# Adjacency layer with residual and layer norm: the bias enters through the self half's cross product, taken by VectorE

## Chip, cores and metric

The kernel runs on one core of a Trainium2 chip. The metric is the device time of one execution in microseconds (us); less is better. A core has TensorE (PE: matmuls, with the weight loads listed apart as PEld), VectorE (DVE), ScalarE (ACT), GpSimd (POOL), SyncE (SP, which only issues DMAs here) and 16 DMA engines.

## What is computed

The reference, cut to what matters (x is 8 x 2048 x 512, adj is 2048 x 2048 of 0 and 1, W is 512 x 1024, all results fp32):

```python
Wi, Wj = (W[:, :Din], W[:, Din:])
mi = jnp.einsum('bkd,od->bko', x, Wi)
mj = jnp.einsum('bkd,od->bko', x, Wj)
deg = a.sum(axis=1)                      # a = adj as float
out = deg[None, :, None] * (mi + b) + jnp.einsum('ij,bjo->bio', a, mj)
return _layernorm(x + out, axis=-1)
```

So there are two projections of x, the neighbour half (mj, h = 0 in the kernel) and the self half (mi, h = 1). The bias b is added to mi before it is multiplied by the degrees.

## The kernel before

The 8 batches of 2048 rows are 128 tiles of 128 rows, 16 to a batch. Each batch has two stages.

**Projection.** TensorE runs its matmuls on numbers of reduced precision, so each operand is cut in a top part and a rest, and three products are made. For tile n and half h, `project(n, s, h, first)` makes 4 matmuls into `cross_ps[h]` (from `x_df` and `W_df`) and then 8 into `main_ps[h]`. The result is main * (1 + 1/S) - cross. There is one PSUM bank for each of `main_ps[0]`, `main_ps[1]`, `cross_ps[0]`, `cross_ps[1]`. ScalarE copies the cross product out (`take_cross(n, 0)`, `take_cross(n, 1)`, into `cross[0]`, `cross[1]`), and VectorE combines (`combine_mj`, `combine_mi`). The neighbour half stays on the chip in `mj_hi` (made by ScalarE) and `mj_lo` (made by GpSimd). The self half goes through one SBUF tile `mi`, which SyncE stores to DRAM (`store_mi`, to `mi_dram`); the next write of `mi` waits until that store has landed (`mi_stored`). VectorE also splits x two tiles ahead (`split_x(n + 2)`: `x_top`, `x_raw`), ScalarE makes `x_hi` and `x_lo` of it (`parts`), and GpSimd `x_df` (`difference`).

**Aggregation.** For each of 16 output tiles TensorE makes 32 matmuls of a widened adjacency tile (`adjT`, by ScalarE's `widen`) with `mj_hi` and `mj_lo` into one of two banks `agg_ps`. SyncE loads `mi` and x back (`mi_in`, `r`), GpSimd adds the bias (`add_bias`), VectorE forms deg * mi + x (`residual`), adds the aggregate and normalises (`normalise`).

**Batch 0** has more to do. The weights come in eight chunks, which VectorE and ScalarE split (`split_w`, `copy_w_hi`), and tiles 0 and 1 (`NATIVE = 2`) are projected "natively" from the unsplit fp32 data, since they can start early. Their self halves are copied out of PSUM by `native_mi(0)` and `native_mi(1)`, on ScalarE, tile 0 from `main_ps[1]` and tile 1 from `cross_ps[1]`. The first split tile is tile 2. Its self-half cross product writes `cross_ps[1]` again, so TensorE waits there for `mi_ready` to reach 2, which is for both native copies (here `h` is 1):

```python
if first:
    pe.wait_ge(mj_ready if h == 0 else mi_ready, NATIVE)
```

Batch 0 also takes in the adjacency matrix, 64 chunks of 128x512 integers in four buffers `adj_in`. Of each chunk ScalarE makes an int8 copy (`cast_chunk`) and VectorE a running sum of degrees (`count_chunk`, `deg_part`); 28 chunks go in the projection stage, two for each tile from tile 2 on, and 36 in the aggregation stage.

Every engine runs its own instruction stream in the written order, and semaphores tie the streams together. SyncE's stream around the two native tiles is: for n in 0, 1: wait for the native matmuls, `load_chunk(2 + n)`, `store_mi(n)`.

Of the kernel before, what the change touches and what calls it, by code (L numbers as in the profile page):

```python
# [5 lines left out]
def bass_adj_resnorm(nc, x, xt, adjt, wt, b, out):  # L6
# [6 lines left out]
    ALU = mybir.AluOpType  # L13
# [5 lines left out]
    P = 128  # L19
# [4 lines left out]
    GT = 4  # L24
# [15 lines left out]
    with ctx:  # L40
# [65 lines left out]
        x_parts_ready = sem("x_parts_ready")  # L106
        x_df_ready = sem("x_df_ready")
        cross_done = sem("cross_done")
        cross_ready = sem("cross_ready")
        main_done = sem("main_done")  # L110
        mj_ready = sem("mj_ready")
        mj_hi_ready = sem("mj_hi_ready")
# [9 lines left out]
        deg_ready = sem("deg_ready")  # L122
        adjT_ready = sem("adjT_ready")
        zeroed = sem("zeroed")
        mib_ready = sem("mib_ready")
        res_ready = sem("res_ready")
        agg_done = sem("agg_done")
        sum_ready = sem("sum_ready")
# [42 lines left out]
        def _(sp):  # L171
# [13 lines left out]
            sp.dma_start(x_first[1], xt[1]).then_inc(x_first_loaded[1], 16)  # L185
            for c in range(DK):
                sp.dma_start(w_stage[c][:, :], wt[c]).then_inc(w_loaded[c], 16)
            for s in range(2):
                sp.dma_start(x_raw[s][:, :], xt[NATIVE + s]).then_inc(x_loaded[s], 16)
            sp.dma_start(bias[:, :], b.partition_broadcast(P)).then_inc(b_loaded, 16)  # L190
            for c in range(2):
                load_chunk(c)
            for n in range(NATIVE):
# [80 lines left out]
        @block.gpsimd  # L274
        def _(pool):
            pool.memset(warm[:, :], 0.0).then_inc(zeroed, 1)
            pool.memset(ones[:, :].bitcast(fp32), 1.0).then_inc(zeroed, 1)

            def difference(n, s):
                pool.wait_ge(x_parts_ready, 2 * (n - NATIVE) + 2)  # L280
                pool.tensor_tensor(x_df[s][:, :], x_top[:, :], x_lo[s][:, :].bitcast(fp32),  # L281
                                   ALU.subtract).then_inc(x_df_ready, 1)

            def rest_of_mj(n, t):
                pool.wait_ge(mj_hi_ready, n + 1)
                pool.tensor_tensor(mj_lo[:, bass.ds(t, 1), :].rearrange("p t d -> p (t d)"), mj[:, :],  # L286
                                   mj_hi[:, bass.ds(t, 1), :].rearrange("p t d -> p (t d)").bitcast(fp32),
                                   ALU.subtract).then_inc(mj_lo_ready, 1)

            def add_bias(m, u, turn):  # L290
                pool.wait_ge(mi_loaded[u % 2], turn)
                pool.tensor_tensor(mi_in[u % 2][:, :], mi_in[u % 2][:, :], bias[:, :], ALU.add).then_inc(mib_ready, 1)  # L292

            difference(NATIVE, 0)

            def batch(bt):
                zero = known(bt) and bt == 0
                final = known(bt) and bt == NB - 1

                def proj(g):  # L300
                    for u in range(GT):
                        if zero and GT * g + u < NATIVE:
                            continue
                        n = NT * bt + GT * g + u
                        if not (final and known(g) and g == NG - 1 and u == GT - 1):
                            difference(n + 1, (u + 1) % 2)
                        rest_of_mj(n, GT * g + u)

                over_groups(pool, zero, final, proj)
                if zero:  # L310
                    pool.wait_ge(b_loaded, 16)
                with pool.Fori(0, NP) as k:
                    for u in range(2):
                        add_bias(NT * bt + 2 * k + u, u, 16 * (NP * bt + k + 1))

            over_batches(pool, batch)

        @block.tensor
        def _(pe):
# [12 lines left out]
            def project(n, s, h, first):  # L332
                half = 1 - h
                if first:
                    pe.wait_ge(w_ready, (h + 1) * DK)
                if h == 0:
                    pe.wait_ge(x_df_ready, n - NATIVE + 1)
                if first:
                    pe.wait_ge(mj_ready if h == 0 else mi_ready, NATIVE)
                else:  # L340
                    pe.wait_ge(cross_ready, 2 * (n - NATIVE) - 1 + h)
                for k in range(DK):
                    last = nc.tensor.matmul(cross_ps[h][:, :], x_df[s][:, k * P:(k + 1) * P],  # L343
                                            W_df[:, half * DK + k, :], start=(k == 0), stop=(k == DK - 1))
                last.then_inc(cross_done, 1)
                if first:
                    pe.wait_ge(w_hi_ready, (h + 1) * DK)
                    pe.wait_ge(w_lo_ready, (h + 1) * DK)
                pe.wait_ge(mj_ready if h == 0 else mi_ready, n)
                for k in range(DK):  # L350
                    nc.tensor.matmul(main_ps[h][:, :], x_hi[s][:, k * P:(k + 1) * P],  # L351
                                     W_hi[:, half * DK + k, :], start=(k == 0), stop=False)
                    last = nc.tensor.matmul(main_ps[h][:, :], x_lo[s][:, k * P:(k + 1) * P],  # L353
                                            W_lo[:, half * DK + k, :], start=False, stop=(k == DK - 1))
                last.then_inc(main_done, 1)
# [66 lines left out]
        def _(act):  # L422
# [6 lines left out]
                nc.scalar.activation(mj_hi[:, n, :], (main_ps if n == 0 else cross_ps)[0][:, :],  # L429
                                     ACT.Copy).then_inc(mj_hi_ready, 1)  # L430

            def native_mi(n):
                act.wait_ge(main_done, NATIVE + n + 1)
                if n:
                    act.wait_ge(mi_stored, 16 * n)
                nc.scalar.activation(mi[:, :], (main_ps if n == 0 else cross_ps)[1][:, :],
                                     ACT.Copy).then_inc(mi_ready, 1)

            def parts(n, s):
                act.wait_ge(x_top_ready, n - NATIVE + 1)  # L440
                if not (known(n) and n < NATIVE + 2):
# [6 lines left out]
                act.wait_ge(x_parts_ready, 2 * (n - NATIVE) - 2)  # L448
                act.dma_start(x_raw[s][:, :], xt[n]).then_inc(x_loaded[s], 16)

            def take_cross(n, h):
                act.wait_ge(cross_done, 2 * (n - NATIVE) + 1 + h)
                act.wait_ge(mj_ready if h == 0 else mi_ready, n)
                nc.scalar.activation(cross[h][:, :], cross_ps[h][:, :], ACT.Copy).then_inc(cross_ready, 1)  # L454

            def top_of_mj(n, t):
                act.wait_ge(mj_ready, n + 1)
# [23 lines left out]
            native_mj_hi(1)  # L481
            parts(NATIVE, 0)
            load_x(NATIVE + 2, 0)
            native_mi(0)
            for order in range(1, DK):
                copy_w_hi(order, DK + order)
            native_mi(1)

            def batch(bt):
                zero = known(bt) and bt == 0  # L490
# [2 lines left out]
                def proj(g):  # L493
                    last_group = known(g) and g == NG - 1
                    for u in range(GT):
                        t = GT * g + u
                        n = NT * bt + t
                        if zero and t < NATIVE:
                            continue
                        if not (final and last_group and u == GT - 1) and (zero or not (known(g) and t == 0)):  # L500
                            parts(n + 1, (u + 1) % 2)
                        take_cross(n, 0)
                        if not (final and last_group and u >= GT - 3):
                            load_x(n + 3, (u + 1) % 2)
                        if zero:
                            for c in proj_chunks(t)[:-1]:
                                cast_chunk(c)
                        take_cross(n, 1)
                        top_of_mj(n, t)
                        if zero:  # L510
                            cast_chunk(proj_chunks(t)[-1])
                        if last_group and u in (0, 2):
                            widen(u // 2, u // 2, NT if zero else None)
# [37 lines left out]
        def _(dve):  # L551
# [29 lines left out]

            def combine_mj(n):
                dve.wait_ge(main_done, 2 * n + 1)
                dve.wait_ge(cross_ready, 2 * (n - NATIVE) + 1)
                if not (known(n) and n == NATIVE):
                    dve.wait_ge(mj_lo_ready, n - NATIVE)
                nc.vector.scalar_tensor_tensor(mj[:, :], main_ps[0][:, :], 1.0 + 1.0 / S, cross[0][:, :],  # L587
                                               ALU.mult, ALU.subtract).then_inc(mj_ready, 1)

            def combine_mi(n):  # L590
                dve.wait_ge(main_done, 2 * n + 2)
                dve.wait_ge(cross_ready, 2 * (n - NATIVE) + 2)
                dve.wait_ge(mi_stored, 16 * n)
                nc.vector.scalar_tensor_tensor(mi[:, :], main_ps[1][:, :], 1.0 + 1.0 / S, cross[1][:, :],  # L594
                                               ALU.mult, ALU.subtract).then_inc(mi_ready, 1)
# [18 lines left out]
                                      deg_ps[:, 0:2 * TPB].rearrange("p (t c) -> p t c", c=2)[:, :, 0]  # L614
                                      ).then_inc(deg_ready, 1)

            def residual(m, i, u, turn):
                dve.wait_ge(mib_ready, m + 1)
                dve.wait_ge(r_loaded[u], turn)
                if known(m) and m < NT:  # L620
                    dve.wait_ge(deg_ready, m // TPB + 1)
# [34 lines left out]
            split_x(NATIVE, 0, 16)  # L656
            for order in range(1, DK):
                split_w(order, DK + order)
            split_x(NATIVE + 1, 1, 16)

            def batch(bt):
                zero = known(bt) and bt == 0
# [2 lines left out]
                def proj(g):  # L665
                    for u in range(GT):
# [7 lines left out]
                        if zero:  # L674
                            for c in proj_chunks(t)[:-1]:
                                count_chunk(c)
                        combine_mi(n)
                        if zero:
                            count_chunk(proj_chunks(t)[-1])
# [2 lines left out]

                over_groups(dve, zero, final, proj)
                base = NT * bt
                residual(base, 0, 0, 16 * (NG * bt + 1))

                def agg(g):
                    for u in range(GT):
# [10 lines left out]
                                take_degrees(3)  # L699
                        ending = known(g) and g == NG - 1 and u == GT - 1  # L700
                        if not ending:
                            residual(m + 1, i + 1, (u + 1) % GT, 16 * (NG * bt + g + 1 + (u + 1) // GT))
                        normalise(m, u, u % 2, final and ending)

                if zero:
# [39 lines left out]
```

## Time and profile before

| | before |
|---|---|
| time, median of 3 runs | 1643.62 us (1643.59 to 1643.74) |
| the profiled execution's own time | 1643.72 us |
| its span in the profile | 1641.9 us |
| TensorE busy | 1634.2 us, 7196 matmuls |
| VectorE busy | 844.8 us, 1879 instructions |
| ScalarE busy | 661.7 us, 964 instructions |
| GpSimd busy | 498.4 us, 386 instructions |
| DMA | 187.27 MB, mean 114 GB/s |

The span runs from the first to the last instruction of the profiled execution; the 1.8 us between it and that execution's time lie around the instructions. Busy time counts instructions that do work, not waits. A matmul of 512 columns shows as 389 ns, but the next one starts 0.23 us later, since they are pipelined. Batch 0's projection ends at about 97 us of the span and its aggregation at about 214 us; each later batch takes 87 us of projection and 116 us of aggregation.

### The profile page before, as it was taken

To read this page: it belongs to the slowest core of one execution; us is meant where nothing else is said; L and a number is where in the kernel's file an instruction comes from. 1 tells how busy PE (TensorE), PEld (TensorE's weight loads), DVE (VectorE), ACT (ScalarE), POOL (GpSimd) and SP (SyncE) were. 2 spreads that over 40 slices of the span, in tenths; PEclk is the share of its full clock that TensorE was granted. 3 is DMA by queue.
4 is the path that set the end of the run, shared out by engine and by line. 5 is a ranking of instruction groups with operands and counts; after the bars stand their busy time and mean duration, and the time that the engine had idled before them with its cause. 6 is when DMAs were issued, how large, how long until landed. Compare 5 with 4: busy or idle time off the path is not lost.

```text
span 1641.9 us, 24654 instructions
## 1 busy us (share of the span) xinstructions
PE 1634.2 (100%) x7196; PEld 1346.8 (82%) x7196; DVE 844.8 (51%) x1879; ACT 661.7 (40%) x964; POOL 498.4 (30%) x386
## 2 busy tenths in 40 slices
PE   9999999999999999999999999999999999999998
PEld 6888888888888888888888888888888888888886
DVE  8787644554444544444544544444544454544544
ACT  5765445332453324532245332452325522255221
POOL 3532134311343114431144211442114421144210
PEclk9999999999999999999999999999999999999999
DMA  6676422332234323243223332233323333233332
GB/s 205 193 226 223 141 84 94 131 108 96 83 102 133 100 93 96 89 134 109 84 95 101 123 115 83 95 114 117 102 83 102 124 106 106 74 101 115 96 115 70
DMA packets 102843, 187.27 MB, mean 114 GB/s; under 512 B 11424, under 2 KB 11680, under 8 KB 102816
## 3 DMA queue, kind: packets, MB, share of 16 engines
q1 hardware_dynamic: 84672, 154.05, 29.1%
q10 hardware_dynamic: 18144, 32.91, 6.3%
q8 instruction: 11, 0.18, 0.0%
q14 instruction: 16, 0.13, 0.0%
HBM read 119.80 MB, written 67.11 MB: 114 GB/s over the span
## 4 chain that ended last, share of the span: by engine, by line
PE 98%; DVE 1%; DMA 0%; issue 0%; POOL 0%; ACT 0%; DVEq 0%
PE agg_ps L375 57%; PE cross_ps L343 14%; PE main_ps L351 14%; PE main_ps L353 14%; DVE W_lo L558 0%; DVE W_df L561 0%; DMA mi_in<-in_wt 0%; DVE adjT L555 0%; DVE x_raw L579 0%; DVE mj_lo L568 0%; PE deg_ps L360 0%; POOL x_df L281 0%; DVE x_top L576 0%; DVE stats L630 0%; DVE r L628 0%
## 5 line engine op out<-in xcount | busy, mean ns | idle before, releaser
L375 PE MATMUL agg_ps<-mj_hi,adjT 128*128 128x512 f32 x2048 | 797.0, 389 | 0.0
L375 PE MATMUL agg_ps<-mj_lo,adjT 128*128 128x512 f32 x2048 | 796.7, 389 | 0.0
L470 ACT ACTIVATE adjT<-adjT 128x2048 fp32r (+1 forms) x128 | 245.4, 1917 | 562.8 <-PE agg_ps L375 562.8
L375 PEld LDWEIGHTS agg_ps<-mj_hi,adjT 128*128 128x128 f32 x2048 | 384.5, 188 | 79.9
L375 PEld LDWEIGHTS agg_ps<-mj_lo,adjT 128*128 128x128 f32 x2048 | 384.3, 188 | 79.7
L351 PE MATMUL main_ps<-W_hi,x_hi 128*128 128x512 f32 x1008 | 392.3, 389 | 0.0
L353 PE MATMUL main_ps<-W_lo,x_lo 128*128 128x512 f32 x1008 | 392.1, 389 | 0.0
L292 POOL TENSOR_TENSOR mi_in<-mi_in,bias 128x512 f32<-128x512 f32 x128 | 166.9, 1307 | 649.9 <-DMA mi_in<-mi_dram 649.9
L628 DVE TENSOR_TENSOR r<-agg_ps,r 128x512 f32<-128x512 f32 x128 | 88.6, 692 | 355.0 <-PE agg_ps L375 354.9
L343 PE MATMUL cross_ps<-W_df,x_df 128*128 128x512 f32 x1008 | 270.2, 390 | 0.6 <-DVE W_df L561 0.5
L286 POOL TENSOR_TENSOR mj_lo<-mj,mj_hi 128x512 f32 (+1 forms) x126 | 166.7, 1323 | 323.4 <-ACT mj_hi L458 323.4
L454 ACT ACTIVATE cross<-cross_ps 128x512 f32<-128x512 f32 x252 | 148.6, 590 | 215.0 <-PE cross_ps L343 213.5
L343 PEld LDWEIGHTS cross_ps<-W_df,x_df 128*128 128x128 f32 x1008 | 189.0, 188 | 40.9 <-DVE W_df L561 0.9
L351 PEld LDWEIGHTS main_ps<-W_hi,x_hi 128*128 128x128 f32 x1008 | 189.3, 188 | 39.8 <-DVE mi L594 0.3
L353 PEld LDWEIGHTS main_ps<-W_lo,x_lo 128*128 128x128 f32 x1008 | 189.1, 188 | 39.2
L281 POOL TENSOR_TENSOR x_df<-x_top,x_lo 128x512 fp32r<-128x512 f32 x126 | 164.9, 1309 | 150.1 <-ACT x_lo L445 149.8
L587 DVE SCALAR_TENSOR_TENSOR mj<-main_ps,cross 128x512 f32<-128x512 f32 x126 | 87.1, 691 | 224.0 <-PE main_ps L353 218.8
L594 DVE SCALAR_TENSOR_TENSOR mi<-main_ps,cross 128x512 f32<-128x512 f32 x126 | 87.0, 691 | 107.6 <-PE main_ps L353 105.7
L622 DVE SCALAR_TENSOR_TENSOR r<-mi_in,deg,r 128x512 f32<-128x512 f32 x128 | 101.4, 796 | 13.1 <-POOL mi_in L292 9.2
L443 ACT ACTIVATE x_hi<-x_top 128x512 fp32r<-128x512 f32 x126 | 79.6, 632 | 63.3 <-PE main_ps L353 61.3
L630 DVE BATCH_NORM_STATS2 stats<-r 128x6 f32<-128x512 f32 x128 | 89.0, 695 | 11.7
L579 DVE TENSOR_TENSOR x_raw<-x_raw,x_top 128x512 f32<-128x512 f32 x126 | 87.3, 693 | 4.3
(59 smaller groups left out, 592.1 us busy)
## 6 DMA issues: line engine op xcount, KB each, us to landing
mi_dram<-mi SPq DMA_DIRECT2D x128, 256.0 KB, 2.1
mi_in<-mi_dram SPq DMA_DIRECT2D x128, 256.0 KB, 2.7
r<-in_x SPq DMA_DIRECT2D x128, 256.0 KB, 2.6
out<-r SPq DMA_DIRECT2D x127, 256.0 KB, 2.1
x_raw<-in_xt ACTq DMA_DIRECT2D x124, 256.0 KB, 2.7
adj_in<-in_adjt SPq DMA_DIRECT2D x64, 256.0 KB, 3.9
r<-in_wt SPq DMA_DIRECT2D x4, 256.0 KB, 5.2
adj_in<-in_xt SPq DMA_DIRECT2D x2, 256.0 KB, 4.0
```

The source lines that it names most:

```text
L281: pool.tensor_tensor(x_df[s][:, :], x_top[:, :], x_lo[s][:, :].bitcast(fp32), ALU.subtract).then_inc(x_df_ready, 1)
L286: pool.tensor_tensor(mj_lo[:, bass.ds(t, 1), :].rearrange("p t d -> p (t d)"), mj[:, :], mj_hi[:, bass.ds(t, 1), :].rearrange("p t d -> p ...
L292: pool.tensor_tensor(mi_in[u % 2][:, :], mi_in[u % 2][:, :], bias[:, :], ALU.add).then_inc(mib_ready, 1)
L343: last = nc.tensor.matmul(cross_ps[h][:, :], x_df[s][:, k * P:(k + 1) * P], W_df[:, half * DK + k, :], start=(k == 0), stop=(k == DK - 1))
L351: nc.tensor.matmul(main_ps[h][:, :], x_hi[s][:, k * P:(k + 1) * P], W_hi[:, half * DK + k, :], start=(k == 0), stop=False)
L353: last = nc.tensor.matmul(main_ps[h][:, :], x_lo[s][:, k * P:(k + 1) * P], W_lo[:, half * DK + k, :], start=False, stop=(k == DK - 1))
L375: last = nc.tensor.matmul(agg_ps[s][:, :], adjT[s][:, j, :], part[:, j, :], start=(j == 0 and part is mj_hi), stop=(j == NT - 1 and part i ...
L454: nc.scalar.activation(cross[h][:, :], cross_ps[h][:, :], ACT.Copy).then_inc(cross_ready, 1)
L470: nc.scalar.activation(adjT[s][:, :, :], adjT8[:, :, bass.ds(i * P, P)], ACT.Copy).then_inc(adjT_ready, 1)
L622: nc.vector.scalar_tensor_tensor(r[u][:, :], mi_in[u % 2][:, :], deg[:, bass.ds(i, 1)], r[u][:, :], ALU.mult, ALU.add).then_inc(res_ready, 1)
L628: nc.vector.tensor_tensor(r[u][:, :], agg_ps[s][:, :], r[u][:, :], ALU.add).then_inc(sum_ready, 1)
L630: nc.vector.bn_stats(stats[:, :], r[u][:, :]).then_inc(ln_step, 1)
```

## The change

The bias no longer is added by GpSimd when `mi` has come back from DRAM. For the split tiles VectorE, and not ScalarE, takes the self half's cross product out of PSUM, and subtracts the bias as it does so; since the result is main minus cross, the stored `mi` then holds the bias. For the two native tiles VectorE, and not ScalarE, copies `mi` out of PSUM and adds the bias. GpSimd's loop of 128 adds and its semaphore `mib_ready` are gone, and `residual` waits for the load of `mi_in` itself. The semaphore `cross_ready` becomes one for each half. The load of the bias is issued two DMAs earlier. No matmul is added, removed or moved.

```diff
@@ SyncE, start
             for c in range(DK):
                 sp.dma_start(w_stage[c][:, :], wt[c]).then_inc(w_loaded[c], 16)
+            sp.dma_start(bias[:, :], b.partition_broadcast(P)).then_inc(b_loaded, 16)
             for s in range(2):
                 sp.dma_start(x_raw[s][:, :], xt[NATIVE + s]).then_inc(x_loaded[s], 16)
-            sp.dma_start(bias[:, :], b.partition_broadcast(P)).then_inc(b_loaded, 16)
@@ GpSimd
-            def add_bias(m, u, turn):
-                pool.wait_ge(mi_loaded[u % 2], turn)
-                pool.tensor_tensor(mi_in[u % 2][:, :], mi_in[u % 2][:, :], bias[:, :], ALU.add).then_inc(mib_ready, 1)
...
-                if zero:
-                    pool.wait_ge(b_loaded, 16)
-                with pool.Fori(0, NP) as k:
-                    for u in range(2):
-                        add_bias(NT * bt + 2 * k + u, u, 16 * (NP * bt + k + 1))
@@ TensorE, project
                 else:
-                    pe.wait_ge(cross_ready, 2 * (n - NATIVE) - 1 + h)
+                    pe.wait_ge(cross_ready[h], n - NATIVE)
@@ ScalarE
-            def native_mi(n):
-                act.wait_ge(main_done, NATIVE + n + 1)
-                if n:
-                    act.wait_ge(mi_stored, 16 * n)
-                nc.scalar.activation(mi[:, :], (main_ps if n == 0 else cross_ps)[1][:, :],
-                                     ACT.Copy).then_inc(mi_ready, 1)
...
-                        take_cross(n, 0)
+                        take_cross(n)
...
-                        take_cross(n, 1)
                         top_of_mj(n, t)
@@ VectorE
+            def native_mi(n):
+                if n == 0:
+                    dve.wait_ge(b_loaded, 16)
+                else:
+                    dve.wait_ge(mi_stored, 16 * n)
+                dve.wait_ge(main_done, NATIVE + n + 1)
+                nc.vector.tensor_tensor(mi[:, :], (main_ps if n == 0 else cross_ps)[1][:, :], bias[:, :],
+                                        ALU.add).then_inc(mi_ready, 1)
+
+            def take_cross_less_bias(n):
+                dve.wait_ge(cross_done, 2 * (n - NATIVE) + 2)
+                dve.wait_ge(mi_ready, n)
+                nc.vector.tensor_tensor(cross[1][:, :], cross_ps[1][:, :], bias[:, :],
+                                        ALU.subtract).then_inc(cross_ready[1], 1)
...
-            def residual(m, i, u, turn):
-                dve.wait_ge(mib_ready, m + 1)
+            def residual(m, i, u, turn, mi_turn):
+                dve.wait_ge(mi_loaded[u % 2], mi_turn)
...
             for order in range(1, DK):
                 split_w(order, DK + order)
+            native_mi(0)
             split_x(NATIVE + 1, 1, 16)
+            native_mi(1)
...
                         if zero:
                             for c in proj_chunks(t)[:-1]:
                                 count_chunk(c)
+                        take_cross_less_bias(n)
                         combine_mi(n)
```

What stands where, as the two built programs have it. The first place is VectorE's stream at the start, from the split of the last weight chunk to the first `mj`. "L555" is a line of the kernel that the row belongs to, `adjT` in the top parts of the weights is their scratch space, and `mi<-main_ps` and `mi<-cross_ps` are the native copies. Before:

```order
L555 TENSOR_SCALAR adjT<-r 128x2x256 [waits w_loaded3]
L558 TENSOR_TENSOR W_lo<-r,adjT 128x512 [waits w_top_ready]
L561 SCALAR_TENSOR_TENSOR W_df<-adjT,W_lo 128x512 [waits w_lo_ready]
L576 TENSOR_SCALAR x_top<-x_raw 128x512 [waits x_df_ready,x_parts_ready,x_loaded1]
L579 TENSOR_TENSOR x_raw<-x_raw,x_top 128x512 [waits x_top_ready]
L587 SCALAR_TENSOR_TENSOR mj<-main_ps,cross 128x512 [waits cross_ready,main_done]
```

And of the changed kernel (its line numbers are its own):

```order
L535 TENSOR_SCALAR adjT<-r 128x2x256 [waits w_loaded3]
L538 TENSOR_TENSOR W_lo<-r,adjT 128x512 [waits w_top_ready]
L541 SCALAR_TENSOR_TENSOR W_df<-adjT,W_lo 128x512 [waits w_lo_ready]
L576 TENSOR_TENSOR mi<-main_ps,bias 128x512 [waits main_done,b_loaded]
L556 TENSOR_SCALAR x_top<-x_raw 128x512 [waits x_df_ready,x_parts_ready,x_loaded1]
L559 TENSOR_TENSOR x_raw<-x_raw,x_top 128x512 [waits x_top_ready]
L576 TENSOR_TENSOR mi<-cross_ps,bias 128x512 [waits main_done,mi_stored]
L567 SCALAR_TENSOR_TENSOR mj<-main_ps,cross 128x512 [waits cross_ready0,main_done]
```

The two native copies now stand on VectorE behind all eight weight chunks, one before and one behind the split of tile 3's x, and the second waits for the store of the first.

The second place is VectorE's stream over one tile of batch 0 (tile 3). Before:

```order
L587 SCALAR_TENSOR_TENSOR mj<-main_ps,cross 128x512 [waits mj_lo_ready,cross_ready,main_done]
L576 TENSOR_SCALAR x_top<-x_raw 128x512 [waits x_df_ready,x_parts_ready,x_loaded1]
L579 TENSOR_TENSOR x_raw<-x_raw,x_top 128x512 [waits x_top_ready]
L608 TENSOR_TENSOR deg_part<-deg_part,adj_in 128x512 [waits deg_part_ready,adj_loaded2]
L594 SCALAR_TENSOR_TENSOR mi<-main_ps,cross 128x512 [waits mi_stored,cross_ready,main_done]
L608 TENSOR_TENSOR deg_part<-deg_part,adj_in 128x512 [waits deg_part_ready,adj_loaded3]
```

And of the changed kernel:

```order
L567 SCALAR_TENSOR_TENSOR mj<-main_ps,cross 128x512 [waits mj_lo_ready,cross_ready0,main_done]
L556 TENSOR_SCALAR x_top<-x_raw 128x512 [waits x_df_ready,x_parts_ready,x_loaded1]
L559 TENSOR_TENSOR x_raw<-x_raw,x_top 128x512 [waits x_top_ready]
L603 TENSOR_TENSOR deg_part<-deg_part,adj_in 128x512 [waits deg_part_ready,adj_loaded2]
L582 TENSOR_TENSOR cross<-cross_ps,bias 128x512 [waits mi_ready,cross_done]
L589 SCALAR_TENSOR_TENSOR mi<-main_ps,cross 128x512 [waits mi_stored,cross_ready1,main_done]
L603 TENSOR_TENSOR deg_part<-deg_part,adj_in 128x512 [waits deg_part_ready,adj_loaded3]
```

One instruction is added, between the two degree counts. Later batches have the same stream without the counts.

## Rows read from the trace of the kernel before

**Rows 1.** The page: busy us (share of the span) and instructions of each engine

```profile
PE 1634.2 (100%) x7196; PEld 1346.8 (82%) x7196; DVE 844.8 (51%) x1879; ACT 661.7 (40%) x964; POOL 498.4 (30%) x386
```

**Rows 2.** Waits of the weight loads: us in total, times, longest

```profile
PEld cross_ps L343 <- DVE W_df L561: 0.9, 1, 0.9
PEld cross_ps L343 <- POOL x_df L281: 0.5, 1, 0.5
...
PEld main_ps L351 <- DVE mi L594: 0.3, 1, 0.3
```

**Rows 3.** Timeline of the start: start us, us, engine, line, what

```profile
20.91 0.58 ACT L436 ACTIVATE mi<-cross_ps 128x512 f32<-128x512 f32 x1
20.97 0.39 PE L353 MATMUL main_ps<-W_lo,x_lo 128*128 128x512 f32 x1
21.09 0.69 DVE L561 SCALAR_TENSOR_TENSOR W_df<-adjT,W_lo 128x512 fp32r<-128x512 f32 x1
21.51 0.34 SPq L180 DMA_DIRECT2D mi_dram<-mi  x1
21.71 0.42 DVE L576 TENSOR_SCALAR x_top<-x_raw 128x512 uint32<-128x512 uint32 x1
...
21.84 1.20 PE L343 MATMUL cross_ps<-W_df,x_df 128*128 128x512 f32 x4 [0.48 <-DVE W_df L561]
...
22.88 0.39 PE L351 MATMUL main_ps<-W_hi,x_hi 128*128 128x512 f32 x1
...
24.95 1.20 PE L343 MATMUL cross_ps<-W_df,x_df 128*128 128x512 f32 x4
...
25.98 0.39 PE L351 MATMUL main_ps<-W_hi,x_hi 128*128 128x512 f32 x1
```

**Rows 4.** DVE at a native tile: an operation with one PSUM source

```profile
13.71 0.68 DVE L568 TENSOR_TENSOR mj_lo<-cross_ps,mj_hi 128x512 fp32r<-128x512 f32 x1
```

**Rows 5.** Stores of mi, issue to landing: issued at 28.25; at 81.06; all 128

```profile
DMA to landing us min/median/max: 5.0/5.0/5.0
...
DMA to landing us min/median/max: 2.3/2.3/2.3
...
DMA to landing us min/median/max: 2.0/2.6/5.8
```

**Rows 6.** SPq: the chunk loads right behind the store issued at 81.06

```profile
81.76 6.04 SPq L176 DMA_DIRECT2D adj_in<-in_adjt  x2
```

**Rows 7.** The last matmul; then stretches (five engines' busy us, granted clock, DMA share, GB/s)

```profile
1635.45 0.39 PE L375 MATMUL agg_ps<-mj_lo,adjT 128*128 128x512 f32 x1
...
1639.00:1640.00 1.00, 0.00 (x0) 0.00 (x0) 0.73 (x2) 0.00 (x0) 0.00 (x0) 0.98 0.00 0
1640.00:1641.00 1.00, 0.00 (x0) 0.00 (x0) 0.00 (x0) 0.00 (x0) 0.00 (x0) 0.50 0.71 243
```

**Rows 8.** Batch 0: DVE and POOL beside each other, in order of time

```profile
27.30 1.47 POOL L281 TENSOR_TENSOR x_df<-x_top,x_lo 128x512 fp32r<-128x512 f32 x1
27.54 0.68 DVE L594 SCALAR_TENSOR_TENSOR mi<-main_ps,cross 128x512 f32<-128x512 f32 x1
...
41.13 1.45 POOL L286 TENSOR_TENSOR mj_lo<-mj,mj_hi 128x512 fp32r<-128x512 f32 x1 [1.91 <-ACT mj_hi L458]
...
41.35 1.78 DVE L608 TENSOR_TENSOR deg_part<-deg_part,adj_in 128x512 fp32r<-128x512 f32 x1
43.05 0.68 DVE L594 SCALAR_TENSOR_TENSOR mi<-main_ps,cross 128x512 f32<-128x512 f32 x1
43.65 1.24 DVE L608 TENSOR_TENSOR deg_part<-deg_part,adj_in 128x512 fp32r<-128x512 f32 x1
```

**Rows 9.** DVE: the self half of a tile in a later batch

```profile
433.82 0.69 DVE L594 SCALAR_TENSOR_TENSOR mi<-main_ps,cross 128x512 f32<-128x512 f32 x1 [0.97 <-PE main_ps L353]
```

**Rows 10.** Waits of DVE: us in total, times, longest

```profile
DVE r L628 <- PE agg_ps L375: 354.9, 123, 3.7
...
DVE r L622 <- POOL mi_in L292: 9.2, 7, 1.3
```

More of the change, by code:

```diff
@@ L108, in bass_adj_resnorm @@
         cross_done = sem("cross_done")
-        cross_ready = sem("cross_ready")
+        cross_ready = [sem(f"cross_ready{h}") for h in range(2)]
         main_done = sem("main_done")
@@ L124, in bass_adj_resnorm @@
         zeroed = sem("zeroed")
-        mib_ready = sem("mib_ready")
         res_ready = sem("res_ready")
@@ L449, in load_x, with take_cross @@
                 act.dma_start(x_raw[s][:, :], xt[n]).then_inc(x_loaded[s], 16)
[L451 to L454, printed above, removed]
+            def take_cross(n):
+                act.wait_ge(cross_done, 2 * (n - NATIVE) + 1)
+                act.wait_ge(mj_ready, n)
+                nc.scalar.activation(cross[0][:, :], cross_ps[0][:, :], ACT.Copy).then_inc(cross_ready[0], 1)
             def top_of_mj(n, t):
@@ L483, in _ @@
             load_x(NATIVE + 2, 0)
-            native_mi(0)
             for order in range(1, DK):
                 copy_w_hi(order, DK + order)
-            native_mi(1)
             def batch(bt):
@@ L583, in combine_mj @@
                 dve.wait_ge(main_done, 2 * n + 1)
-                dve.wait_ge(cross_ready, 2 * (n - NATIVE) + 1)
+                dve.wait_ge(cross_ready[0], n - NATIVE + 1)
                 if not (known(n) and n == NATIVE):
@@ L588, in combine_mj @@
                                                ALU.mult, ALU.subtract).then_inc(mj_ready, 1)
+            def native_mi(n):
[11 more added lines that the diff above has]
+                                        ALU.subtract).then_inc(cross_ready[1], 1)
             def combine_mi(n):
                 dve.wait_ge(main_done, 2 * n + 2)
-                dve.wait_ge(cross_ready, 2 * (n - NATIVE) + 2)
+                dve.wait_ge(cross_ready[1], n - NATIVE + 1)
                 dve.wait_ge(mi_stored, 16 * n)
@@ L684, in batch @@
                 base = NT * bt
-                residual(base, 0, 0, 16 * (NG * bt + 1))
+                residual(base, 0, 0, 16 * (NG * bt + 1), 16 * (NP * bt + 1))
                 def agg(g):
@@ L701, in agg @@
                         if not ending:
-                            residual(m + 1, i + 1, (u + 1) % GT, 16 * (NG * bt + g + 1 + (u + 1) // GT))
+                            residual(m + 1, i + 1, (u + 1) % GT, 16 * (NG * bt + g + 1 + (u + 1) // GT),
+                                     16 * (NP * bt + 2 * g + (u + 1) // 2 + 1))
                         normalise(m, u, u % 2, final and ending)
```

## The prediction

> **What bounds the kernel now.** I read the table of busy time first. TensorE is busy for 1634.2 of the 1641.9 us of the span [rows 1], and 7196 matmuls in that time are 0.227 us each. Nothing in the change touches a matmul, so what can move is only the time in which TensorE does nothing: the start, the tail behind the last matmul, and any wait between. The waits of the weight loads come next, because an engine that is held at a semaphore shows it there. Behind the issue gaps of the native tiles there are three waits on another engine, of 0.9, 0.5 and 0.3 us [rows 2], all in the first 35 us; later TensorE waits for nobody. VectorE on the other hand waits 354.9 us for TensorE in the aggregation stage, and 9.2 us for GpSimd's bias add [rows 10]. So the 128 adds that leave GpSimd (about 1.3 us each) are worth nothing in time by themselves: they stand in an engine that nobody on the path waits for, and the 9.2 us lie inside VectorE's idle time. The question is whether work that VectorE takes on makes TensorE wait.
>
> **Part 1: the aggregation stage.** `residual` waits for the load instead of GpSimd, so it comes earlier. It is hidden before and after by TensorE's 32 matmuls for each tile (7.26 us). Value: nothing. The tail behind the last matmul has no bias in it either and stays.
>
> **Part 2: one VectorE operation more for each split tile.** `take_cross_less_bias` reads one operand from PSUM and one from SBUF; the nearest row is the native `mj_lo`, 0.68 us [rows 4], and operations of this kind follow each other at 0.60 us (43.05 to 43.65 in [rows 8]). ScalarE gets rid of as much. In a later batch VectorE sits idle for 0.97 us just ahead of `mi` [rows 9], when the cross product of that half has long been done (it ends 1.81 us, 8 matmuls, ahead of the main one). The new operation fits in that gap. Value: nothing, seven batches out of eight.
>
> Batch 0 is tighter. A tile lasts 24 x 0.227 = 5.44 us on TensorE. VectorE has `mj`, `x_top`, the rest of x, a count, the new operation, `mi` and a count: six at 0.60 and one at 0.45, 4.05 us. The counts can be held up: beside GpSimd's `mj_lo` (started at 41.13) the count of 41.35 let the next operation in only at 43.05, 1.70 us later instead of 0.60, and a count behind `x_df` takes 1.24 instead of 0.69 [rows 8]. With both, a tile costs 4.05 + 1.10 + 0.55 = 5.70 us, 0.26 more than TensorE needs. I still cost it at nothing. First, there is slack: counted from the start of a tile, `mj` can start at 2.9 us, the new operation at 6.25 with a held-up count and it ends at 6.93, and TensorE wants the bank `cross_ps[1]` again only at 8.16. Second, the lateness doesn't add up: GpSimd's `x_df` is timed by TensorE (through `x_hi`, which waits for the main product), so the count held up behind it ends at a fixed time after TensorE's, and VectorE is at most about 0.5 us late for the next `mj`. The cover is thus 0.7 to 1.2 us; without it a tile would cost 0.26 us.
>
> Would the new operation be held up by GpSimd too? `mi<-main_ps,cross` has the same kinds of operand, started at 27.54 under a GpSimd operation that ran from 27.30 to 28.77, and took 0.68 us [rows 8]. So I add 0.60 and no more. The Trainium skill, page "SBUF — State Buffer", says that VectorE and GpSimd hold a shared pair of ports exclusively, for a VectorE operation with two SBUF inputs against a GpSimd operation that reads SBUF; the trace agrees (1.24 and 1.78 us for the counts, 0.68 for a PSUM source). Had the rule covered the new operation as well, another 1.10 us for each of 14 tiles would come on top, some 15 us less 1 us of slack.
>
> **Part 3: the start, where the sum is made.** Tile 2's self half may write `cross_ps[1]` only when both native `mi` are out. Before, ScalarE had the second one out at 21.49, just ahead of the last weight chunk, for which TensorE waited anyway: the last `W_df` ends at 21.78 and the cross product starts at 21.84 [rows 3]. Now VectorE comes to the first copy only behind that `W_df`, and the second copy needs the store of the first to land, a round trip that nothing hides any longer. Step by step:
>
> First copy: `W_df` starts at 21.09, the next operation 0.61 later, at 21.70; 0.68 us [rows 4]; done at 22.38. (The bias was asked for in the first 6 us and is no limit.) The store is issued 0.02 us behind, as before (21.49 to 21.51 [rows 3]): 22.40.
>
> Landing: all 128 stores take 2.0 at the least, 2.6 in the median, 5.8 at most. Here the DMA engines are nearly idle, and one chunk load follows 0.35 us behind the store, since `load_chunk(3)` stands behind `store_mi(0)` on SyncE. The store of 81.06 had chunk loads right behind it and took 2.3 [rows 5, 6]. I take 2.3, between the ends 2.0 and 5.0: 24.70.
>
> Second copy: VectorE meanwhile splits tile 3's x (from 22.30 to about 23.4), so that isn't late. Some 0.1 us to wake and 0.68 us: done at 25.50. TensorE starts 0.06 later, at 25.56, which is 3.72 us later than 21.84.
>
> From there 1.04 us to the first main matmul (21.84 to 22.88 [rows 3]) and 8 x 0.227 = 1.82 us bring the next cross product to 28.42. Before, it started at 24.95 after 0.25 us of waiting for `x_df` [rows 2, 3], and its first main matmul came at 25.98. Now `x_df` is there (its chain is 0.6 us later, done at about 25.5), and without a restart the first main matmul of tile 3 comes 4 x 0.227 = 0.91 later, at 29.33. The difference is 29.33 - 25.98 = 3.35 us.
>
> Everything behind is TensorE at its pace, so these 3.35 us reach the end. VectorE's backlog is not worse: `mj` of tile 2 runs at 25.4, 1.3 us later than before, while TensorE is 3.4 us later. One small thing goes the other way: the 0.3 us wait of the main matmuls for `mi` [rows 2] came from a store that took 5.0 us to land [rows 5] and cost TensorE 0.15 us at 34.3. It may vanish, or another such store may cost the same somewhere in batch 0; I leave both out and keep 0.15 for the range.
>
> **Sum.** +3.4 us in place of nothing, rounded up for the wake of VectorE that no row shows. The profiled execution had a span of 1641.9 and a time of 1643.72, 0.1 above the median of the three: span 1645.3, time 1643.62 + 3.4 = 1647.0 us. About 0.2%, 3.3 us here, is what a measurement of this kernel can tell from no change, so the sum lies just on that bound.
>
> **The rivals.** The store lands fast, and nothing can be measured. With 2.0 us, and without the stall of 0.15 us, the sum is 3.35 - 0.30 - 0.15 = 2.9 us, 1646.5. For it: the start has few DMAs under way. Against it: only the least of 128 stores lands that fast. It decides from a landing of about 2.2 us down.
>
> The clock drops in the new gap. TensorE's last matmul before the gap ends at 21.36 and the next starts at 25.56: 4.2 us. At the kernel's end the granted clock was still whole until about 1639.96 (0.98 for the stretch up to 1640, then 0.50, the 1.2 GHz level), 4.1 us behind the last matmul at 1635.84 [rows 7]. So the gap is as long as the one idle time that is shown to bring the clock down. If it falls, the matmuls behind run at twice their 0.227 us until it is given back; no row shows how long that is, between nothing and some us. If it lasts as long as the fall took, 4.1 us, half of it is lost: +2.05, 1649.1 us. Against it: the fall would have to come in the last instants of the gap. The Trainium skill, page "TensorE: Matmul & The Clock Gate", section "Part 1: The HAM clock gate", says that an idle TensorE goes back to its half-rate state, and warns of idle gaps of this order between bursts of matmuls. By that rule alone the forecast would be 1649 rather than 1647.
>
> VectorE becomes the bound in batch 0. If the counts are held up in every tile and lateness does add up, 14 tiles x 0.26 = 3.6 us less 1.2 us of slack, +2.4: 1649.4 us. For it: 5.70 against 5.44. Against it: `x_df` is tied to TensorE, as said above.
>
> **How the numbers follow.** The forecast (landing over 2.2 us, nothing else) has 0.45, with a range of its own of 1646.8 to 1648.0. The fast landing has 0.31, the clock 0.12, VectorE in batch 0 0.08, and 0.04 stay for what I don't see, most of it slower, 0.02 faster. Slower by over 0.2% is the forecast but for a 0.07 at its lower edge, the clock, VectorE and the rest: 0.60. Within 0.2%: 0.31 + 0.07 = 0.38. Faster: 0.02, since nothing on TensorE's path is taken away but waits that sum to 0.5 us. The range goes from 1646.4, a landing of 2.0 us, to 1649.3, the clock and a part of VectorE; 0.2 is left outside.
>
> **What would show it.** Right: one wait of some 4 us of TensorE ahead of its second cross product by `W_df`, released by VectorE's native `mi`, which itself waited for the DMA of `mi_dram`; an idle VectorE of about 1.2 us there; tile 3's first main matmul at 29.3; then no wait of TensorE over 0.3 us; a granted clock of 1.00 in 22 to 35 us; VectorE's busy time up by 128 x 0.69 = 88 us, ScalarE's down by 75, GpSimd's by 167. Wrong: the second native copy before 24.4 or behind 26 (landing), matmuls 0.43 us apart behind 25.5 (clock), or waits of the cross products for `cross<-cross_ps,bias` in batch 0 (VectorE).

## The result and the profile after

The changed kernel takes 1648.18 us in the median of 11 executions (1646.61 to 1649.44), the kernel before 1643.74 (11 executions, 1643.48 to 1644.05). The ratio is 1.0026, interval 1.0018 to 1.0034: slower by 4.4 us. Its executions don't lie in one place: three are at 1646.6 to 1646.9, seven at 1648.1 to 1648.5, one, the profiled, at 1649.4. Those of the kernel before lie within 0.6 us. The mean granted clock over the whole execution is 0.999 in the three, 0.998 in the seven and 0.997 in the one; 3.4 us at half the clock in 1646 us take 0.001 off that mean, so the groups differ by such stretches.

The page of the profiled execution, busy time of each engine (it answers to [rows 1]):

```profile
PE 1635.9 (99%) x7196; PEld 1348.6 (82%) x7196; DVE 918.6 (56%) x2007; ACT 598.8 (36%) x836; POOL 333.6 (20%) x258
```

Its waits of TensorE's matmuls, us in total, times, longest (the weight loads, whose waits [rows 2] gives, list this one under "issue"). The three waits of [rows 2] were 0.9 us at most:

```profile
PE cross_ps L333 <- DVE mi L576: 4.4, 1, 4.4
```

TensorE has the same 7196 matmuls and one wait of 4.4 us on a native copy, now on VectorE (L576 in the changed kernel is `native_mi`). The timeline of the start shows the chain that leads there, in the columns of [rows 3]:

```profile
20.68 0.39 PE L343 MATMUL main_ps<-W_lo,x_lo 128*128 128x512 f32 x1
...
21.17 0.69 DVE L541 SCALAR_TENSOR_TENSOR W_df<-adjT,W_lo 128x512 fp32r<-128x512 f32 x1
21.78 0.68 DVE L576 TENSOR_TENSOR mi<-main_ps,bias 128x512 f32<-128x512 f32 x1
...
22.49 0.34 SPq L179 DMA_DIRECT2D mi_dram<-mi  x1
...
24.60 0.69 DVE L576 TENSOR_TENSOR mi<-cross_ps,bias 128x512 f32<-128x512 f32 x1 [1.07 <-DMA mi_dram<-mi]
...
25.44 2.05 PE L333 MATMUL cross_ps<-W_df,x_df 128*128 128x512 f32 x4 [4.37 <-DVE mi L576]
27.28 0.63 PE L341 MATMUL main_ps<-W_hi,x_hi 128*128 128x512 f32 x1
27.71 0.63 PE L343 MATMUL main_ps<-W_lo,x_lo 128*128 128x512 f32 x1
```

First copy, store, landing (2.1 us), second copy, TensorE: as forecast, within 0.2 us at each step. But then the matmuls follow each other at 0.43 us, where 0.23 is usual, and the granted clock says why (stretches; busy us of the five engines, granted clock, DMA share, GB/s; it answers to [rows 7]):

```profile
22.00:24.00 2.00, 0.00 (x0) 0.00 (x0) 1.49 (x3) 1.07 (x2) 0.00 (x0) 1.00 0.34 125
24.00:25.00 1.00, 0.00 (x0) 0.00 (x0) 0.40 (x1) 1.00 (x3) 0.73 (x1) 0.69 0.88 258
25.00:26.00 1.00, 0.56 (x1) 0.50 (x2) 1.00 (x3) 0.31 (x2) 0.53 (x1) 0.50 0.68 100
...
30.00:31.00 1.00, 1.00 (x4) 0.81 (x3) 0.07 (x1) 0.01 (x1) 0.00 (x0) 0.50 0.42 162
31.00:32.00 1.00, 1.00 (x5) 0.77 (x5) 1.00 (x2) 1.00 (x2) 0.00 (x0) 0.89 0.00 0
```

The clock fell to 1.2 GHz at 24.4 us (0.69 over 24 to 25 is 0.62 us at half), 3.3 us behind the last matmul, and stayed there until 31.2. TensorE worked for 5.8 us of that. A matmul took 0.43 us there in place of 0.23, so 0.20/0.43, a little under half of the 5.8 us, is lost: 2.7 us. The span is 1647.6 us, 5.7 more than before: 2.7 of them the clock, 3.0 the wait. So the loss has two terms, and only one of them is in every execution.

In the aggregation stage VectorE's wait of 9.2 us for GpSimd is gone, and its wait for TensorE, 354.9 us before [rows 10], has grown by more than that; the time saved there is idle time:

```profile
DVE r L623 <- PE agg_ps L365: 373.4, 124, 5.3
```

### The profile page after: what moved, and what is told of

It reads as the page before. It is cut to its first block, busy times and chain, and to the rows that moved or that the text cites. A ratio compares the mean times of both kernels' runs of the same rounds, so it can differ in the third digit from the quotient of the medians.

```text
span 1647.6 us, 24322 instructions
## 1 busy us (share of the span) xinstructions
PE 1635.9 (99%) x7196; PEld 1348.6 (82%) x7196; DVE 918.6 (56%) x2007; ACT 598.8 (36%) x836; POOL 333.6 (20%) x258
## 4 chain that ended last, share of the span: by engine, by line
PE 98%; DVE 1%; DMA 0%; issue 0%; DVEq 0%; ACT 0%
PE agg_ps L365 56%; PE cross_ps L333 14%; PE main_ps L343 14%; PE main_ps L341 14%; DVE W_lo L538 0%; DVE W_df L541 0%; DMA mi_in<-in_wt 0%; DVE adjT L535 0%; DMA mi_dram<-mi 0%; DVE mi L576 0%; DVE mj_lo L548 0%; PE deg_ps L350 0%; DVE stats L625 0%; DVE x_raw L559 0%; DVE r L623 0%
## 5 line engine op out<-in xcount | busy, mean ns | idle before, releaser
L441 ACT ACTIVATE mj_hi<-mj 128x512 fp32r<-128x512 f32 (+1 forms) x126 | 79.8, 633 | 234.1 <-DVE mj L567 234.1
L617 DVE SCALAR_TENSOR_TENSOR r<-mi_in,deg,r 128x512 f32<-128x512 f32 x128 | 94.9, 746 | 3.1 <-issue 2.5
L582 DVE TENSOR_TENSOR cross<-cross_ps,bias 128x512 f32<-128x512 f32 x126 | 86.0, 683 | 0.4 <-PE cross_ps L333 0.4
```

The costliest lines, as they stand in the source:

```text
L617: nc.vector.scalar_tensor_tensor(r[u][:, :], mi_in[u % 2][:, :], deg[:, bass.ds(i, 1)], r[u][:, :], ALU.mult, ALU.add).then_inc(res_ready, 1)
```

## The experiments

The numbers are medians, with the extremes of the executions. The kernel before, run beside them, had a median of 1643.71 (32 executions, 30 of them within 1643.5 to 1644.4, two at 1644.9 and 1645.1) for the first four, and 1643.67 (15 executions) for the next three, which ran on another chip. An "interval" is the 95% interval of the ratio.

**1. The native copies back on ScalarE.** GpSimd adds the bias of tiles 0 and 1 alone; the other 126 tiles are as in the change.

```diff
@@ ScalarE
+            native_mi(0)
             for order in range(1, DK):
                 copy_w_hi(order, DK + order)
+            native_mi(1)
@@ VectorE
-            native_mi(0)
             split_x(NATIVE + 1, 1, 16)
-            native_mi(1)
@@ GpSimd, behind the projection of batch 0
+                    for m in range(NATIVE):
+                        pool.wait_ge(mi_loaded[m], 16)
+                        pool.tensor_tensor(mi_in[m][:, :], mi_in[m][:, :], bias[:, :], ALU.add).then_inc(mib_ready, 1)
```

> The changed kernel with only the two native copies put back on ScalarE, ahead of their old places; GpSimd adds the bias for tiles 0 and 1 alone, when they have come back from DRAM. The extra VectorE operation for the 126 split tiles stays. Theory (all of the loss is the wait of the second split cross product for the native copies, with the clock that falls in it): TensorE's long wait is gone and the time is that of the kernel before, 1643.7 us, within 0.2 us. Rival (VectorE's extra operation costs TensorE something in batch 0 or later): 1644.5 us or more.

Measured: 1644.31 us (1644.16 to 1644.49, 11 executions), ratio 1.0004, interval 0.9994 to 1.0013. 3.9 of the 4.4 us are gone, and the spread with them, but 0.6 us stay: between the two expectations. The interval does not exclude "no change", but all eleven executions lie above 28 of the 32 of the kernel before, so the 0.6 us are taken as real. The waits of this kernel's TensorE name it:

```profile
PE cross_ps L339 <- DVE cross L588: 0.3, 1, 0.3
```

And its timeline of VectorE shows what was ahead of the take:

```profile
26.29 1.52 DVE L606 CAST deg_part<-adj_in 128x512 fp32r<-128x512 int32 x1
27.73 0.68 DVE L588 TENSOR_TENSOR cross<-cross_ps,bias 128x512 f32<-128x512 f32 x1
```

The first split tile's take stands behind a count that a GpSimd operation (25.74 to 27.52) holds up, and TensorE, which now isn't late, comes for the bank before it is free. In the changed kernel this costs nothing, as TensorE is 3 us late there anyway.

**2. Only the native copies moved.** The kernel before, with `native_mi` on VectorE at the places of the change, as a plain copy; GpSimd still adds every bias.

```diff
@@ VectorE
+            native_mi(0)
             split_x(NATIVE + 1, 1, 16)
+            native_mi(1)
```

> The kernel before with only the two native copies moved from ScalarE to the places on VectorE where the changed kernel has them; everything else, GpSimd's bias adds too, as before. Theory: the whole loss comes back, +3.0 us in executions whose clock stays whole and +4.4 us and more in the others, so 1646.7 to 1649.4 us, median near 1648.2. Rival (the loss is of several parts): under 1646 us.

Measured: 1648.29 us (1646.73 to 1648.54, 10 executions), ratio 1.0026, interval 1.0016 to 1.0035. The two copies alone bring the whole loss, with both its terms. In its profile TensorE waits 3.9 us, the clock falls at 26.0 and is back at 29.4.

**3. Without the wait for the store.** The second copy goes to `cross[1]`, which is free until the first take, and is stored from there.

```diff
-                else:
-                    dve.wait_ge(mi_stored, 16 * n)
...
+                nc.vector.tensor_tensor((mi if n == 0 else cross[1])[:, :], (main_ps if n == 0 else cross_ps)[1][:, :], bias[:, :],
@@ take_cross_less_bias
+                if known(n) and n == NATIVE:
+                    dve.wait_ge(mi_stored, 32)
```

> The changed kernel, but the second native copy goes to the free tile cross[1] and is stored from there, so it needs no store to land; the first split tile's take waits for that store. Theory: the second copy starts right behind the split of tile 3's x, at about 23.5 us instead of 24.6, TensorE's idle stretch falls from 4.4 to 3.3 us, and the part of the loss that is waiting falls from 3.0 to about 1.9 us: 1645.6 us where the clock stays whole, at times 1 to 2 us more. Rival (the landing isn't what sets it): same as the changed kernel.

Measured: 1645.77 us in the median, with seven executions at 1645.5 to 1645.8 and four at 1647.1; ratio 1.0015, interval 1.0006 to 1.0024. The wait's share is 1.9 us instead of 3.0, as worked out. The store's round trip is thus 1.1 us of the loss, and the other 1.9 us come from the place of the copies in VectorE's stream. The profiled execution, one of the seven, waited 2.1 us, and its clock stayed whole; the expectation had 3.3 us, but TensorE's last matmul before the gap ended at 22.39 there and not at 21.07. The mean granted clock is 0.999 in the seven and 0.998 in the four.

**4. The gap filled.** 16 matmuls with nothing to do, ahead of the waiting cross product, in the changed kernel.

```diff
                 half = 1 - h
+                if first and h == 1:
+                    for k in range(16):
+                        nc.tensor.matmul(agg_ps[0][:, :], x_hi[s][:, 0:P], W_hi[:, DK, :], start=True, stop=True)
```

> The changed kernel with 16 idle-time matmuls of 512 columns (3.6 us, into a bank that nobody reads until it is written anew) ahead of the waiting cross product; the wait itself stays. Theory (waiting and clock are two terms): the granted clock is 1.00 throughout, every execution comes to +3.0 us, 1646.7, with no spread beyond 0.3 us. Rival (the spread of the changed kernel has another cause): the median stays at 1648.2 with executions from 1646.6 to 1649.4.

Measured: 1646.97 us, ten of eleven executions at 1646.7 to 1647.3, one at 1648.2; ratio 1.0019, interval 1.0010 to 1.0028. The wait is unchanged (the cross product starts at 25.47), the granted clock is 1.00 in every stretch of the profile and 0.999 or 1.000 on average in all eleven executions, and 1.2 us of the median's loss are gone. That is the second term by itself. The spread of the ten, 0.6 us, is twice what was expected. The execution at 1648.2 has a mean clock of 1.000, so the clock isn't its cause; it has no profile, and two of the kernel before were nearly as far off.

**5. The take ahead of the count.** Kernel 1 with one thing changed: VectorE's take stands before the tile's first count.

```diff
+                        take_cross_less_bias(n)
                         if zero:
                             for c in proj_chunks(t)[:-1]:
                                 count_chunk(c)
-                        take_cross_less_bias(n)
```

> The kernel of the native copies on ScalarE (1644.3 us, in whose trace TensorE waited 0.3 to 0.7 us for the first take of a cross product, at 28.5 us, behind a degree count that GpSimd had held up for 0.8 us), but on VectorE the take stands ahead of the tile's first count instead of behind it. Theory (that one wait is the 0.6 us that this kernel still lost): 1643.7 us, as before the change. Rival (the 0.6 us are lost elsewhere): 1644.3 us still.

Measured: 1643.58 us (1643.39 to 1644.37, 11 executions), ratio 0.9999, interval 0.9990 to 1.0008. The waits of the profiled execution have no take in them any more, and the median is that of the kernel before: the 0.6 us were that one wait. (The profiled execution is the slowest of the eleven, 1644.37. Its matmuls wait 0.5 us for a `mi` whose store took 5.6 us to land, the kind of small stall that the prediction kept for its range.) In this form the change costs nothing and gains nothing: the bias adds of the 126 split tiles are gone from GpSimd, and the time is that of the kernel before.

**6. The take twice.** Kernel 1 with each take made a second time.

```diff
+                nc.vector.tensor_tensor(cross[1][:, :], cross_ps[1][:, :], bias[:, :],
+                                        ALU.subtract).then_inc(taken_once, 1)
+                dve.wait_ge(taken_once, n - NATIVE + 1)
```

> The kernel of the native copies on ScalarE, but VectorE takes each self-half cross product twice, one behind the other (0.75 us more for each split tile). Theory (the later batches have the room, 0.97 us ahead of mi before the change less 0.6 us for the first take and 2.0 us ahead of mj; batch 0 has not): only batch 0 loses. Its VectorE pitch was 5.35 us for a tile; 6.1 us against TensorE's 5.44 would cost 0.66 us for each of 14 tiles less some 1.5 us of slack: up to +7 us, 1651 us; if the counts fall out of step with GpSimd, 5.55 us a tile and +1 us, 1645.5 us. Rival (all batches lose): 0.3 us or more for each of 126 tiles, 1680 us or more.

Measured: 1652.29 us (1652.0 to 1652.7, 5 executions), ratio 1.0052, 8.0 us above kernel 1, a little over the upper case. Its waits of the weight loads:

```profile
PEld cross_ps L340 <- DVE cross L592: 10.1, 12, 1.5
```

Its timeline of VectorE, the first counts of two tiles in a row:

```profile
32.19 1.79 DVE L613 TENSOR_TENSOR deg_part<-deg_part,adj_in 128x512 fp32r<-128x512 f32 x1
...
38.27 1.78 DVE L613 TENSOR_TENSOR deg_part<-deg_part,adj_in 128x512 fp32r<-128x512 f32 x1
```

A tile takes VectorE 6.08 us, TensorE waits for 12 takes, all in batch 0, and what a tile takes over 5.44 us is paid: 0.64 us in each of some 13 tiles is 8.3. The later batches have no such wait. Kernel 1, in the same view, needs 5.38 and 5.34 us for a tile. The view shows no idle time of VectorE in it, but `mi` starts 0.77 us behind the take whose result it reads, and not 0.60:

```profile
31.36 1.79 DVE L609 TENSOR_TENSOR deg_part<-deg_part,adj_in 128x512 fp32r<-128x512 f32 x1
...
34.48 0.68 DVE L609 TENSOR_TENSOR deg_part<-deg_part,adj_in 128x512 fp32r<-128x512 f32 x1
...
36.74 1.78 DVE L609 TENSOR_TENSOR deg_part<-deg_part,adj_in 128x512 fp32r<-128x512 f32 x1
38.44 0.68 DVE L588 TENSOR_TENSOR cross<-cross_ps,bias 128x512 f32<-128x512 f32 x1
39.21 0.69 DVE L595 SCALAR_TENSOR_TENSOR mi<-main_ps,cross 128x512 f32<-128x512 f32 x1
...
42.08 1.78 DVE L609 TENSOR_TENSOR deg_part<-deg_part,adj_in 128x512 fp32r<-128x512 f32 x1
```

**7. Four filling matmuls** in place of 16, otherwise the edit of kernel 4.

> The changed kernel with 4 idle-time matmuls of 512 columns (0.9 us) instead of 16 at the head of the gap, which leaves 2.2 to 3.5 us of it. Theory (waiting 3.0 us in every execution; the clock term depends on how long TensorE is left idle): between the two, most executions at 1646.8 us and some at 1648.3. Rival (any gap of some us brings the clock down): median at 1648.2 as in the changed kernel.

Measured: 1648.93 us in the median of 1647.15, 1648.26, 1648.93, 1649.35 and 1651.88; ratio 1.0035. This went against the theory: a shorter gap didn't save the clock. The profiled execution (1647.15) waited 2.2 us with a whole clock. Three of the others have a mean granted clock of 0.997 to 0.998 against 0.999; the one at 1648.26 has 1.000, so its 1.1 us come from something else. The one at 1651.88 has 0.997, as has the profiled execution of the changed kernel, where the clock cost 2.7 us; by that estimate about 2 of its 5 us above 1646.9 come from elsewhere too.

**8 to 10. A second profile** of the changed kernel, of kernel 3 and of kernel 7, for the clock. Each is a single execution.

> The changed kernel once more, for a second profile of the gap: how long TensorE is idle, whether and when the granted clock falls, how long it stays low, and what the execution takes. Theory: waiting is worth 3.0 us; the rest of the time above the kernel before is half of the stretch in which the clock is low while TensorE works (first profile: low from about 24.4 to 31.2 us, TensorE working for 5.8 us of it, 2.9 us).

> The kernel without the wait for the store once more, as a look: it took 1645.5 to 1645.8 in 7 executions and 1647.1 in 4. Theory: an execution at 1647.1 shows the lower clock for some 3.4 us of work, one at 1645.6 doesn't; if the length of the gap alone decides, the low one has the longer gap (2.1 us in the first profile, whose clock stayed whole).

> The kernel with 4 filling matmuls once more, as a look: 1647.2 to 1651.9 in 5 executions. Theory: what is above 1646.9 is time at the lower clock; the profile shows for how long, and how long the gap was before it fell (2.2 us in the first profile, whose clock stayed whole).

Measured: 1648.22, 1647.19 and 1648.02 us (the kernel before, once beside them: 1644.70). All three show the fall. Kernel 3's (number 9) is the telling one; first its timeline:

```profile
21.15 0.39 PE L343 MATMUL main_ps<-W_lo,x_lo 128*128 128x512 f32 x1
24.24 1.16 PE L333 MATMUL cross_ps<-W_df,x_df 128*128 128x512 f32 x4 [2.70 <-DVE cross L574]
```

Then its stretches, in the columns above:

```profile
24.00:25.00 1.00, 0.76 (x3) 0.67 (x4) 0.35 (x2) 1.00 (x3) 0.76 (x1) 1.00 0.83 268
25.00:26.00 1.00, 1.00 (x5) 0.81 (x4) 0.78 (x2) 0.74 (x2) 0.53 (x1) 0.82 0.94 258
26.00:27.00 1.00, 1.00 (x3) 0.75 (x3) 0.97 (x3) 0.62 (x2) 0.82 (x1) 0.50 0.73 266
...
29.00:30.00 1.00, 1.00 (x5) 0.81 (x5) 1.00 (x2) 0.98 (x3) 0.16 (x1) 0.97 0.68 70
```

TensorE was idle for 2.7 us, went back to work at 24.24, and the clock fell behind that: 0.82 over 25 to 26 is 0.36 us at half, so it fell at 25.6, and it was back at 29.1. The seven profiles with a gap side by side, each with the clock's stretch worked out in this way:

| kernel | TensorE idle | clock at 1.2 GHz | TensorE at work in it | time |
|---|---|---|---|---|
| changed | 21.07 to 25.44, 4.4 | 24.4 to 31.2 | 5.8 us | 1649.44 |
| changed (8) | 21.24 to 25.39, 4.2 | 25.2 to 28.6 | 3.2 us | 1648.22 |
| 2 | 21.73 to 25.59, 3.9 | 26.0 to 29.4 | 3.4 us | 1648.54 |
| 7 (10) | 21.96 to 25.32, 3.4 | 24.8 to 28.3 | 2.9 us | 1648.02 |
| 3 (9) | 21.54 to 24.24, 2.7 | 25.6 to 29.1 | 3.4 us | 1647.19 |
| 7 | 23.18 to 25.39, 2.2 | not at all | 0 | 1647.15 |
| 3 | 22.39 to 24.44, 2.1 | not at all | 0 | 1645.77 |

0.20/0.43 of the fourth column taken from the time leaves 1646.7 to 1647.0 for the changed kernel and kernel 2, 1646.7 and 1647.2 for kernel 7, and 1645.6 and 1645.8 for kernel 3: the two terms add up to each time within 0.5 us. (The expectation for number 8 took a plain half; the pace of the matmuls makes it somewhat less.) The end of the gap is set by VectorE and hardly moves within a kernel; its start does, by 1.3 us, with the stretch in which the weights and the native tiles come in.

## Why the prediction was right or wrong

The range and the sign were right, and the mechanism of the likeliest case was: the native copies, two small operations, are the whole loss (kernel 2), and the other 126 takes are free in the changed kernel. The number, 1647.0, was 1.2 us low, and the step that failed was the chance of a rival, the clock.

**The wait.** Forecast: 3.35 us, or 3.2 without the small stall. Measured: 3.0 in the executions with a mean clock of 0.999 (1646.61, 1646.71, 1646.91), 3.3 with the gap filled. The second copy started at 24.60 and not 24.8, since the store took 2.1 us and not 2.3. This term was sized right.

**The clock.** "The fall would have to come in the last instants of the gap" gave this rival 0.12. It happened in eight of the eleven executions, by their mean clocks, at a cost of 1.5 us in seven and 2.7 in one, against the 2.05 that the rival had. The step was wrong in its reading of [rows 7]: one idle time that ended in a fall after 4.1 us was taken as the time that a fall needs. The five falls above came 2.9 to 4.3 us behind the last matmul, two of them when TensorE was at work again, and a gap of 2.7 us was enough. The Trainium skill, page "TensorE: Matmul & The Clock Gate", section "Part 1: The HAM clock gate", warned of idle gaps of the length that was forecast, 4.2 us. The traces agree, with a fall at each of the four profiled gaps of 3.4 to 4.4 us, and show one at a gap of 2.7 us as well. That warning should have had more weight than the one row: by it the forecast would have been 1649, 0.8 us off instead of 1.2.

**The aggregation stage and the later batches.** Right: nothing, and with the take doubled still nothing (kernel 6).

**Batch 0.** The value, nothing, was right for the changed kernel; the reasons were half right. Of the two counts in a tile only one is held up for long: that one and the take push the second behind the end of `x_df`. So a tile costs 5.34 to 5.38 us and not 5.70 (kernel 1): the 4.05 us, 1.10 for the one count, and some 0.18 that the sum left out, since the take holds up `mi` for 0.77 us and not 0.60 (38.44 to 39.21). But lateness does add up once a tile is dearer than 5.44: kernel 6 paid 0.64 us tile after tile, where the text had `x_df` put an end to it. What the text called a cover of 0.7 to 1.2 us is eaten up in two tiles then, the room that lasts is 0.1 us a tile, and at the first split tile there is none when TensorE comes in time (kernel 1, 0.6 us). The rival with VectorE as the bound, 0.08, was nearer than it was taken for.

**The take under GpSimd.** Right: in kernel 1 it took 0.68 us at 27.73, while a GpSimd operation ran from 27.48 to 28.95. The counts beside GpSimd's operations took longer, as in [rows 8].

**The other signs.** VectorE waited 1.07 us for the store (forecast: about 1.2), and in kernel 4, whose clock stayed whole, tile 3's first main matmul started at 29.19 (forecast: 29.3). The busy times moved the way that was forecast, by other amounts: VectorE's by 74 us and not 88, ScalarE's by 63 and not 75, GpSimd's by 165 and not 167. For VectorE the forecast multiplied the length of one operation, 0.69 us, by 128, while operations that follow each other come 0.60 us apart and overlap in these views.

**What stays open.** What decides whether the clock falls. The length of the gap alone is not shown to: three executions of the changed kernel kept a whole clock, and by an estimate from the latest start of a gap in any profile (22.39) and the end of theirs (25.4) they too had a gap of about 3.0 us, longer than the 2.7 us of number 9. They have no profile. Why the low clock lasted 3.4 us in four profiles and 6.8 in one. What made the executions of kernel 7 at 1648.26 and 1651.88, the first with a whole clock, and the stray ones of kernel 4 and of the kernel before.

## What to carry to other kernels

Work that leaves an idle engine is worth nothing, and the place where it lands in another engine's stream can be worth a lot: two copies of 0.7 us, set behind a chain that is already the bound and with a DMA round trip between them, cost 3.0 us. Of a one-time wait ask what it lets happen on the engine that waits; here the clock put 1.5 us on top in most executions. When an engine takes one operation more, count its work per tile against the pace of the bound in the busiest stage, with the hold-ups that are there now: 5.4 against 5.44 is no cover for the next change.

## What the runs showed of the hardware

In seven profiles TensorE's granted clock fell to 1.2 GHz with idle stretches of 2.7 to 4.4 us (five of them), and not with 2.1 and 2.2 us. The fall came up to 1.4 us behind the moment when TensorE was at work again (24.24 and 25.6 in number 9), so a profile can show a short gap, some matmuls at full speed, and then 3.4 us at half. One kernel then has executions at several distinct times, 1646.7, 1648.2 and 1649.4 us, with mean clocks of 0.999, 0.998 and 0.997, where the kernel before has one. The gap's start also moves from one execution to the next, by 1.3 us in these profiles; that this is what decides between the times is not shown.
